# Adding the residual stream to a light MLP branch: on GpSimd from a copied buffer, or on TensorE by identity matmuls

## The reference

```python
light_out = feedforward(x, gamma_l, w1_l, b1_l, w2_l, b2_l)      # d_light = 64
s = jnp.einsum('bnd,d->bn', x, routing_token)
scores = coor_descent(s, N_ITERS, effective_k, EPS)              # 50 iterations
selected_scores, selected_indices = jax.lax.top_k(scores, NUM_HEAVY)
routed = jnp.take_along_axis(x, selected_indices[..., None], axis=1)
routed_out = feedforward(routed, gamma_h, w1_h, b1_h, w2_h, b2_h)  # d_heavy = 512
heavy_out = jnp.zeros_like(x).at[batch_range, selected_indices].set(routed_out)
...
x = x + light_out + heavy_out
```

## Time and profile before

| what | value |
|---|---|
| median of 3 runs | 416.61 us (416.41 to 416.74) |
| the profiled execution | 418.83 us |
| its span, first to last instruction | 417.0 us |
| mean granted TensorE clock | 0.947 of full speed |
| busy: PE, DVE, ACT, POOL | 86%, 78%, 63%, 36% of the span |
| from the first `down` matmul (373.09) to the end of the span | 43.9 us |

### The profile page before, as it was taken

How to read it: one execution, slowest core, us unless ns; L and a number is a source line. 1 busy time by engine, 2 the same in 40 slices (tenths; PEclk the granted TensorE clock), 3 DMA queues, 4 the chain that set the end, 5 groups by cost and what they waited for, 6 DMA issues and landing times.

```text
span 417.0 us, 9462 instructions
## 1 busy us (share of the span) xinstructions
PE 358.1 (86%) x3182; PEld 209.9 (50%) x3182; DVE 324.4 (78%) x899; ACT 262.4 (63%) x582; POOL 149.0 (36%) x248
## 2 busy tenths in 40 slices
PE   2788999999999787799968499999989989899791
PEld 1554445444444366379857323444444434456591
DVE  7778699988996338236886497989999997558896
ACT  2245688888888546564553316887877887676630
POOL 8515544665200013001132433356476322451120
PEclk9998899999999969899998956999999999999996
DMA  6432143124430000000000331221311300000003
GB/s 216 114 100 54 53 126 80 42 53 116 118 95 1 2 0 3 0 2 0 2 2 1 89 96 44 59 54 46 78 34 47 78 2 4 0 2 1 2 0 101
DMA packets 35732, 19.98 MB, mean 48 GB/s; under 512 B 4054, under 2 KB 34694, under 8 KB 35686
## 3 DMA queue, kind: packets, MB, share of 16 engines
q1 hardware_dynamic: 34886, 17.81, 16.1%
q10 hardware_dynamic: 608, 1.18, 0.8%
q0 software_dynamic: 192, 0.39, 0.3%
HBM read 5.58 MB, written 1.05 MB: 16 GB/s over the span
## 4 chain that ended last, share of the span: by engine, by line
PE 55%; DVE 26%; ACT 7%; issue 6%; POOL 2%; SPq 2%; DMA 1%; DVEq 0%; ACTq 0%; POOLq 0%
DVE negmax_sb L847 12%; PE pv_ps L1257 11%; PE s_ps L1211 10%; PE prep_ps L1167 4%; PE s_ps L1312 3%; DVE late_sb L1088 3%; PE s_ps L1324 3%; ACT probT_sb L573 2%; PE s_ps L1220 2%; PE prep_ps L1171 2%; PE s_ps L1373 2%; PE prep_ps L1194 2%; PE s_ps L1521 2%; PE out_ps L1356 2%; PE out_ps L1286 2%
## 5 line engine op out<-in xcount | busy, mean ns | idle before, releaser
L847 DVE TENSOR_REDUCE negmax_sb<-s_ps 128x2 bf16<-128x512 f32 x256 | 162.6, 689 | 21.7 <-PE s_ps L1220 21.6
L573 ACT ACTIVATE probT_sb<-s_ps 128x512 f32<-128x512 f32 x256 | 142.3, 597 | 32.0 <-PE s_ps L1211 29.8
L1211 PE MATMUL s_ps<-stack_sb 63*128 63x256 bf16 x512 | 91.4, 279 | 7.3 <-ACT probT_sb L573 3.0
L1220 PE MATMUL s_ps<-stack_sb 62*128 62x256 bf16 x512 | 93.8, 286 | 3.9 <-DMA stack_sb<-parts_sb 3.3
L1257 PE MATMUL pv_ps<-probT_sb,v_aug_sb 128*32 128x256 f32 x1024 | 70.2, 393 | 0.5 <-ACT probT_sb L573 0.5
L1211 PEld LDWEIGHTS s_ps<-stack_sb 63*128 63x128 bf16 x512 | 31.1, 95 | 65.7 <-ACT probT_sb L573 40.2
L449 POOL TENSOR_SCALAR rstd_sb<-mv_sb 128x2 f32<-128x2 f32 x32 | 7.1, 222 | 118.6 <-DVE mv_sb L816 118.6
L595 ACT ACTIVATE qkf_sb<-prep_ps,b_qkv_sb 128x256 f32<-128x256 f32 x56 | 23.9, 471 | 27.4 <-PE prep_ps L1171 20.1
L1257 PEld LDWEIGHTS pv_ps<-probT_sb,v_aug_sb 128*32 128x32 f32 x1024 | 27.1, 110 | 26.5 <-issue 15.1
L1220 PEld LDWEIGHTS s_ps<-stack_sb 62*128 62x128 bf16 x512 | 31.1, 96 | 11.5 <-DVE negmax_sb L847 6.0
L907 DVE SCALAR_TENSOR_TENSOR x_all_sb<-out_ps,den_inv_sb,x_all_sb 128x128 f32<-128x128 f32 x32 | 9.8, 346 | 26.5 <-PE out_ps L1356 26.2
(11 more groups left out here) (186 smaller groups left out, 660.8 us busy)
## 6 DMA issues: line engine op xcount, KB each, us to landing
stack_sb<-parts_sb SPq DMA_DIRECT2D x186, 64.0 KB, 2.1
x_all_sb<-x SPq DMA_DIRECT2D x4, 256.0 KB, 3.0
ctxT_sb<-ctxT ACTq DMA_DIRECT2D x2, 512.0 KB, 6.5
f_w_sb<-f_w SPq DMA_DIRECT2D x2, 512.0 KB, 3.8
out<-x_all_sb SPq DMA_DIRECT2D x4, 256.0 KB, 2.4
d_w_sb<-d_w SPq DMA_DIRECT2D x2, 320.0 KB, 4.2
w_att_sb<-w_att SPq DMA_DIRECT2D x2, 256.0 KB, 4.3
stack_sb<-maxrow_sb ACTq DMA_DIRECT2D x32, 4.0 KB
```

Of the source, the lines that this page charges most:

```text
L573: act.activation(probT[:, c % 8], s2_ps[c % 2][:, :, :], ACT.Exp, scale=DH ** -0.5).then_inc(exp_ready, 1)
L847: dve.tensor_reduce(negmax[:, n % 2, :, max_column(max_head(h))], s1_ps[c % 3][:, :, :], axis=AX.X, op=ALU.max, negate=True).then_inc(max_ ...
L1211: i = pe.matmul(s2_ps[c % 2][:, k, :], stack[rows, s3, 1, h // 2, k * P:(k + 1) * P], stack[rows, s3, 0, h // 2, :], start=True, stop=True)
L1220: i = pe.matmul(s1_ps[c % 3][:, k, :], stack[rows, s3, 0, hp, k * P:(k + 1) * P], stack[rows, s3, 1, hp, :], start=True, stop=True)
```

## The change

Per batch the four records at L1526 (two matmuls against the identity) are gone, and the light product alone goes to the light bank. ScalarE copies that bank no longer to `x_all` but to one of two slots in `prob`, and from the third batch on it waits until GpSimd has emptied the slot. GpSimd, once the heavy and the light copy are there, adds the slot to `x_all` and then, as before, the heavy bias to `heavy`. VectorE's last loop waits for this addition (`light_added`) in place of the copy. TensorE no longer waits for the light bias.

```diff
+        def light_copied(b):
+            return prob[:, b % 2, :, 0:D]
...
             for b in range(B):
                 pool.wait_ge(heavy_copied, b + 1)
+                pool.wait_ge(light_done, b + 1)
+                x2 = x_all[:, last_tiles(b), :]
+                pool.tensor_tensor(x2, x2, light_copied(b), ALU.add).then_inc(light_added, 1)
                 h2 = heavy[:, NT * b:NT * b + NT, :]
                 pool.tensor_tensor(h2, h2, d_b2[:, 0:1, :].broadcast_to([P, NT, D]), ALU.add).then_inc(heavy_ready, 1)
...
                     act.wait_ge(d_y_psum, 2 * b + 2)
-                    act.activation(x_all[:, last_tiles(b), :], light_bank(b), ACT.Copy).then_inc(light_done, 1)
+                    if b >= 2:
+                        act.wait_ge(light_added, b - 1)
+                    act.activation(light_copied(b), light_bank(b), ACT.Copy).then_inc(light_done, 1)
...
                         dve.wait_ge(heavy_ready, b + 1)
-                        dve.wait_ge(light_done, b + 1)
+                        dve.wait_ge(light_added, b + 1)
...
-                    pe.wait_ge(light_bias, b + 1)
                     for k in range(NT):
-                        pe.matmul(light_bank(b)[:, k, :], ident[:, :], x_all[:, last_tiles(b).start + k, :], start=True, stop=False)
                         i = pe.matmul(light_bank(b)[:, k, :], d_hT[:, q % 2, NC - 1, toks[k]], d_w2[:, NC - 1, :],
-                                      start=False, stop=True)
+                                      start=True, stop=True)
```

More of the change, by code:

```diff
@@ L245, in build @@
         xr_ready, xrT_psum, xrT_ready, light_bias = sem("xr_ready"), sem("xrT_psum"), sem("xrT_ready"), sem("light_bias")
-        d_h_psum, d_h_ready, d_y_psum, light_done, heavy_copied, heavy_ready = (
-            sem("d_h_psum"), sem("d_h_ready"), sem("d_y_psum"), sem("light_done"), sem("heavy_copied"), sem("heavy_ready"))
+        d_h_psum, d_h_ready, d_y_psum, light_done, light_added, heavy_copied, heavy_ready = (
+            sem("d_h_psum"), sem("d_h_ready"), sem("d_y_psum"), sem("light_done"), sem("light_added"), sem("heavy_copied"), sem("heavy_ready"))
         shift_step, pick_step, score_step = sem("shift_step"), sem("pick_step"), sem("score_step")
```

## The result

| | before | changed |
|---|---|---|
| median of 9 runs each | 416.61 us (414.81 to 417.75) | 419.80 us (417.60 to 421.05) |
| ratio | 1 | 1.0072 (95% interval 1.0042 to 1.0101) |
| profiled execution, its span | 418.83, 417.0 us | 421.05, 419.2 us |

What follows compares the result with a forecast made beforehand. VectorE's chain of dependent steps was taken to bound the last block, with a 1.45 us wait for ScalarE's second exponential. The terms 1.78 - 0.95 + 1.42 - 0.15 = +2.1 us gave 418.7 us, range 417.1 to 421.1.

Steps and rivals of the forecast that it cites:

- What bounds the block: Last block: VectorE's dependent steps set the end; TensorE can give back only what the second exponential's 1.45 us wait holds.
- The cap of 0.95: Ahead of the second exponential: the most that TensorE's relief of 3.6 us could gain, 0.95 us.
- First block, +1.78: VectorE's first block of steps: eight stretched steps in place of three, 5 x 0.355 = 1.78 us more.
- Wait for the exponential, -0.95: Between the two blocks: the 1.45 us wait shrinks to 0.5 us as ScalarE's table is in earlier, gaining 0.95 us.
- Second block +1.42, weights -0.15: Second block: four more stretched steps, +1.42 us; operations making the weights: meetings fall from 0.6 to 0.45 us, -0.15.
- the weights' price: Operations making the weights: additions cost 0.6 us before, and batch 7's pair 0.45 us (0.18 and 0.27) afterwards.
- The sum: Whole kernel: all terms together make it 2.1 us slower, 418.7 us.
- Held out through both additions of a pair: Rival, VectorE's steps: GpSimd keeps VectorE out through both additions; sum +4.9 us, up to 421.5 us; 13%.
- A pair costs once: Rival, VectorE's steps in both blocks: two additions stretch one step; -0.4 us in sum, 416.2 us; 9%.
- Faster: Rival, VectorE's steps: new additions cost nothing more and the 0.95 us gain remains; 415.7 us; 7%.
- 13 to 15 long steps: Sign in the profile after: VectorE's iteration has 13 to 15 steps over 0.8 us in place of 5.

Runs made afterwards that it cites:

- e1: Changed kernel with the identity matmuls kept but multiplying zeros, so TensorE is not relieved; first step to last loop 36.49 us, ratio to before 1.0090.
- e2: Kernel before without its identity matmuls, no addition on GpSimd in their place; first step to last loop 33.42 us, ratio to before 0.9984.
- e8: Changed kernel with both GpSimd additions of each batch cut into four of 128x64; first step to last loop 31.67 us, ratio to before 0.9955.
- e10: Kernel before with each heavy bias cut into four additions of 128x64, ScalarE's order unchanged; first step to last loop 33.10 us, ratio to before 0.9965.
- e3: Changed kernel with 11 useless matmuls in the last GELU group to keep TensorE busy; first step to last loop 36.69 us, ratio to before 1.0062.
- e4: Kernel before with its eight heavy biases on GpSimd replaced by one-element memsets; first step to last loop 32.85 us, ratio to before 0.9956.
- e0: Changed kernel run again unaltered, compared with the kernel before; first step to last loop 36.85 us, ratio to before 1.0054.
- e9: Changed kernel with both GpSimd additions of each batch cut into two of 128x128; first step to last loop 34.11 us, ratio to before 0.9989.

## Why the prediction was right, point by point

- **What bounds the block**: right. VectorE's chain sets the end, TensorE's 3.6 us are worth nothing at the end of the changed kernel (e1), and the second exponential caps what they could be worth (e2, 0.74). The cap of 0.95 is not fixed: it was the wait behind three stretched steps, and where no step is stretched the relief takes 1.78 from it (e8 against e10).
- **First block, +1.78**: +1.86, eight long steps for three. The price was sized at 0.355: seven of them lost 0.35, one 0.54, a case for which the rows of before had no example (below).
- **Wait for the exponential, -0.95**: -0.96. The number is right, its ascription half so: I booked it as TensorE's gain, but e1 has the same short wait without it, because a row that is late enough hides the table load by itself.
- **Second block +1.42, weights -0.15**: +0.54 and +1.31. This is the step that failed: "ScalarE's GELUs start 0.83 later as well ... and TensorE then gains 0.44 a batch again: pairs from 400.7". A relieved TensorE that waits for GELUs of a late exponential stands idle for 5.2 us and comes back at half clock; the pair came at 402.85, 10.4 us behind the second block's first step, where the forecast had 7.8. With the clock held (e3), the two terms are +1.37 and +0.25, near the forecast. The sum of the two is +1.85 in the changed kernel and +1.62 in e3, for +1.27 forecast. That the wrong split hardly shows in the total is partly luck: the late additions found operations of the weights to hold, which the forecast didn't reckon with.
- **The term that was too small** is the weights' price: in e3 the weights take 4.83, against 3.99 when nothing meets them (e4): 0.84 for batch 7's pair, where I had 0.45; what I had for before, 0.6, is right (4.58 less 3.99). In the changed kernel four operations are stretched by 0.35 to 0.54 and a fifth, L1121, by 0.13 as before. One of the four is L1130, with one tensor input in SBUF, 0.70 where it took 0.33; I had counted only those with two.
- **The sum**: +2.1 forecast, +2.75 measured in the block; whole runs, by the ratio, +3.0 (1.7 to 4.2), and +2.3 in the second comparison (e0). Of the missing 0.65, 0.2 is the half clock and 0.4 the weights.
- **Held out through both additions of a pair**: refuted, by the rows of 0.82 in turn with the additions; no step was longer than 1.05. **A pair costs once**: refuted by eight long steps for eight additions in the first block. **Faster**: refuted for the changed kernel; the relief pays only where the new additions are absent (0.74 in e2) or small (1.78 in e8 against e10). The forecast set against **a pair costs once** that an addition reads for some 0.66 us. No row shows that figure; the shortest addition takes 0.72 in all, and with it the argument is the same.
- 13 to 15 long steps were forecast, 11 found; with the clock held there are 14. TensorE's busy time was to fall by 3.6 us and fell by 1.2: in the 5.5 us at half clock behind the idle time the matmuls took longer, by some 2.7 us as an estimate from the clock of 0.50.

## What to carry to other kernels

Before work moves from an engine with slack to GpSimd, ask whether VectorE runs a chain of dependent operations beside it: each GpSimd addition that met this chain added to it, however idle GpSimd was. If the work has to be there, cut it into pieces and look at what a meeting then costs; here four pieces of 128x64 in place of one of 128x256 took the price for a step from 0.35 us to none. That one piece then fits between the reads of two steps is the likely reason, argued from the three lengths and not seen. The pieces aren't free for everything: in e8 several operations of the weights lost 0.06 to 0.13 us each beside them and those of the last loop 0.05, and GpSimd itself became late. And a short wait measured ahead of a stage is no proof that the engine it waited for got faster; here it was that the other side had become slower.

## What the runs showed of the hardware that I had not expected

- By the profile's start times, the step that starts first doesn't always keep GpSimd out. In e2 a step started at 384.62, 0.01 us ahead of an addition (384.63), and lasted 1.02, until 0.29 behind the addition's end; at 378.16 one that started 0.06 ahead kept the addition waiting. The Trainium skill (SBUF — State Buffer, Who interferes with whom) says that the order of issue decides who is blocked. The second row agrees; the first doesn't, unless the real order there is hidden in the 0.01 us.
- TensorE's clock doesn't go by the length of the idle time alone. It fell to 0.50 after 5.17 us of waiting (changed), 3.79 (e2), 3.57 (e9) and 2.48 (e8, where the stretch from 390 to 395 has a mean of 0.66), and held at 1.00 after 2.99 (e1) and 2.48 (before). What else decides stays open.
- An operation of VectorE's with one tensor input in SBUF (L1130, 8x256) was stretched from 0.33 to 0.70 beside an addition.
